# GpSimd's products two slots earlier in a pipelined block of attention, feed-forward and a selective scan, with a new table of places for the side work

## The chip, the cores and the metric

The kernel runs on one core of a Trainium2 chip. The metric is the device time of one launch in microseconds. Engines are named as in the profile: PE (TensorE), DVE (VectorE), ACT (ScalarE), POOL (GpSimd), SP (SyncE, which here only issues DMAs).

## What is computed

The input is 16 sequences of 512 tokens with 256 features. Each goes through four stages, each with a layer norm ahead and a residual behind. All but the scan can be cut to a few words; the scan sets the frame:

```python
x = x + attention(layernorm(x))      # 16 heads, squared scores, causal
x = x + int8_ffn(layernorm(x))
x = x + mamba_f(norm(x)) + mamba_b(norm(x) reversed)    # two directions
x = x + fp4_ffn(layernorm(x))        # blockwise quantised activations
...
def step(h, ins):                    # 512 inner features, 16 states, 512 tokens
    dt_t, u_t, B_t, C_t = ins
    h = jnp.exp(dt_t[..., None] * A) * h + (dt_t * u_t)[..., None] * B_t[:, None, :]
    y_t = jnp.einsum('bdn,bn->bd', h, C_t)
    return (h, y_t)
```

## The kernel before

One sequence at a time goes through the scan; its work is cut into 128 **slots**, one for each scan instruction of DVE (L1296, 128 features by 512 tokens). A slot belongs to direction r (0 forward, slots 0 to 63; 1 backward, 64 to 127), state s (four slots each, 32 states in all) and feature group m. Every engine runs its own program, slot by slot (`one(b)` on each engine); they meet at semaphores only. In each slot an engine does first its part of the scan and then its **side work**. The part of the scan, in slot j:

- SP issues the spread of row B of a state over all partitions (L688, `spread_b`), for the state of slot j + 7, into a ring of two buffers `bS`.
- POOL makes the products B * dt * u (L786, `inflow`), two slots' worth in one instruction, for slots j + 4 and j + 5. They go into a ring of four buffers `hb`, so the first one of state s waits until PE has transposed all of state s - 4 (`m_hT`).
- ACT makes the decay (L1017) of slot j + 2.
- DVE scans slot j.
- PE transposes the scanned state to token order (L1598, `turn_state`), one quarter per slot, 6 slots behind (slot j - 6), into two PSUM banks.
- DVE adds the first two quarters of each state into y (L1307) 7 slots behind; ACT multiplies the other two by C (L1025) 8 slots behind, and POOL adds them (L797, `add_last`) 9 slots behind.

Side work is everything else: attention and int8 feed-forward of the next sequence, fp4 feed-forward of the one before, the projections ahead of the scan and behind it. The table `PLAN`, filled by `row(piece, r, ahead, PE=[...], ACT=[...], ...)`, gives the slot of every part of a piece on each engine; the whole part of a number is the slot, and within a slot parts go by the number and then by the order of the rows. An engine takes its side work strictly in that order, and so a part that waits holds up all behind it, the next slot's part of the scan too.

Pieces that matter here: `p_in`, `p_conv` (projection and convolution, DVE L1250), `p_silu` (ACT L953 with a table load before and the load L837 behind), `p_x` (PE L1541, then the copy `xd`, ACT L962), `p_c`, `p_rows` (SP L677 writes `xd` out for the spreads) and `p_dt`: the step sizes, for each of four groups a product on PE (L1554), five instructions on ACT (L968 to L977), one on DVE (L1261) and three on POOL (L767, L770, L772). `p_du` is ACT L982. `q_gate`, `q_up`, `q_silu`, `q_hquant`, `q_htail`, `q_hturn`, `q_down` are the fp4 feed-forward (PE L1487, L1506, L1515; ACT L924, L928; DVE L1227, L1073 to L1084; POOL L741 to L747). The norms are `a_stat`/`a_norm` for attention, `f_` for int8, `m_` for the scan, `q_` for fp4: a statistic on DVE (L1124 to L1131), a root on ACT (L843, L845), four tiny instructions on DVE (L1137 to L1143, 128x4 elements) and four scalings on ACT (L851). `a_turn`, `a_k`, `a_v`, `a_q` (PE L1357, L1378, L1365, L1391) make the inputs of attention. `a_score` is PE L1411 and ACT L886, `a_mask` POOL L732. `i_turn`, `d_turn`, `d_gate`, `d_out` (PE L1560, L1570, L1579) close a direction.

## Time and profile before

| | us |
|---|---|
| median of 3 runs | 6269.05 (6259.05 to 6270.88) |
| profiled execution, its own time | 6267.12 |
| its span, first to last instruction | 6265.4 |
| busy: DVE, POOL, PE, ACT | 4807.9, 4688.4, 4489.1, 4183.9 |
| share of the span | 77%, 75%, 72%, 67% |
| mean granted clock of PE, full speed 1 | 0.864 |

A group row of the profile names the line, the engine, the operation and its tiles, then the count, the busy time and the mean duration in ns of one, and last the idle time of the engine before these instructions with what ended it. Nearly all buffers of the scan lie in `arena_m`, and those of the side work in `arena_a`, so lines tell more than tiles. Times in a timeline are from the span's start. The sequence used below begins its slot 0 at 2462.8 us and ends at 2838.4.

### The profile page before, as it was taken

How to read it: one execution, taken by the hardware profiler on the slowest of the kernel's cores; microseconds unless marked ns; L12 is line 12 of the kernel's file. 1: busy time of each engine (PE TensorE's matmuls, PEld its weight loads, DVE VectorE, ACT ScalarE, POOL GpSimd, SP SyncE). 2: the span in 40 equal slices, each digit the busy share in tenths (PEclk: the TensorE clock that was granted, in tenths of full speed). 3: DMA queues.
4: the chain of work that ended last, by engine and by line, in shares of the span. 5: the costliest groups of instructions: out<-in, count | busy, mean ns of one | idle time of the engine just before them, and what ended most of it. 6: DMA issues, size and time to landing. Idle time of an engine off the chain costs nothing. (4 is left out here: it accounts for less than half of the span.)

```text
span 6265.4 us, 79937 instructions
## 1 busy us (share of the span) xinstructions
PE 4489.1 (72%) x21853; PEld 2872.4 (46%) x21900; DVE 4807.9 (77%) x6052; ACT 4183.9 (67%) x7079; POOL 4688.4 (75%) x2442
## 2 busy tenths in 40 slices
...
GB/s 121 36 46 44 46 53 46 53 42 43 62 47 44 46 64 42 45 52 47 55 42 51 55 47 42 57 55 42 43 54 44 55 42 58 50 45 45 39 45 28
DMA packets 152786, 308.71 MB, mean 49 GB/s; under 512 B 20870, under 2 KB 58310, under 8 KB 149926
## 3 DMA queue, kind: packets, MB, share of 16 engines
...
q14 instruction: 294, 2.41, 0.1%
...
## 5 line engine op out<-in xcount | busy, mean ns | idle before, releaser
L786 POOL TENSOR_TENSOR arena_m<-bS,arena_m 128x1024 f32<-128x1024 f32 x1024 | 2429.0, 2383 | 400.6 <-PE psum L1598 349.2
L1296 DVE TENSOR_TENSOR_SCAN arena_m<-psum,arena_m 128x512 f32<-128x512 f32 x2048 | 2441.3, 1208 | 85.2 <-POOL arena_m L786 33.6
L1598 PE MATMUL psum<-ident,arena_m 128*128 128x128 f32 x8192 | 1426.2, 309 | 1020.4 <-ACT hc L1025 762.6
L1598 PEld LDWEIGHTS psum<-ident,arena_m 128*128 128x128 f32 x8192 | 1066.9, 158 | 1662.2 <-issue 889.8
L1017 ACT ACTIVATE psum<-arena_m,Aneg 128x512 f32<-128x512 f32 x2048 | 1400.2, 693 | 520.9 <-DVE arena_m L1296 508.2
L797 POOL TENSOR_TENSOR arena_m<-arena_m,hc 128x1024 f32<-128x1024 f32 x512 | 1213.6, 2370 | 307.3 <-ACT hc L1025 306.5
L1307 DVE SCALAR_TENSOR_TENSOR arena_m<-psum,Ct,arena_m 128x512 f32<-128x512 f32 x1024 | 751.8, 734 | 395.8 <-PE psum L1598 392.2
L1025 ACT ACTIVATE hc<-psum,Ct 128x512 f32<-128x512 f32 x1024 | 697.0, 681 | 62.3 <-PE psum L1598 61.5
L886 ACT ACTIVATE arena_a<-psum 128x512 f32<-128x512 f32 (+3 forms) x1024 | 386.4, 441 | 412.5 <-PE psum L1411 368.7
L1411 PE MATMUL psum<-arena_a 64*128 64x512 f32 (+3 forms) x2048 | 464.4, 559 | 190.9 <-ACT arena_a L886 78.2
L1487 PE MATMUL psum<-wB,arena_a 128*128 128x352 f32 x1024 | 396.4, 519 | 26.4 <-ACT arena_m L992 24.4
L732 POOL TENSOR_SCALAR_AFFINE_SELECT arena_a<-arena_a 128x512 f32<-128x512 f32 x256 | 161.3, 645 | 328.4 <-ACT arena_a L886 328.4
L1250 DVE SCALAR_TENSOR_TENSOR arena_m<-psum,convw,arena_m 128x509 f32<-128x509 f32 (+2 forms) x384 | 285.1, 742 | 130.6 <-ACT arena_m L948 122.6
L741 POOL TENSOR_TENSOR arena_a<-arena_a 128x704 f32<-128x704 f32 (+1 forms) x80 | 144.8, 1810 | 310.8 <-DVE arena_a L1084 310.8
L1411 PEld LDWEIGHTS psum<-arena_a 64*128 64x128 f32 x2048 | 204.2, 225 | 331.9 <-issue 133.3
L1261 DVE SCALAR_TENSOR_TENSOR arena_m<-psum,arena_m 128x512 f32<-128x512 f32 x128 | 88.0, 688 | 343.0 <-ACT arena_m L977 343.0
L1452 PE MATMUL psum<-arena_a,wA 128*128 128x512 bf16 x1105 | 285.4, 404 | 81.5 <-DVE arena_a L1189 74.8
L1524 PE MATMUL psum<-xnT,wU 128*128 128x512 f32 x512 | 265.6, 644 | 31.3 <-DVE arena_m L1250 28.4
L1579 PE MATMUL psum<-wO,arena_m 128*128 128x256 f32 x1024 | 249.8, 388 | 6.0 <-DVE xF L1279 1.7
L1487 PEld LDWEIGHTS psum<-wB,arena_a 128*128 128x128 f32 x1024 | 197.1, 212 | 115.6 <-issue 65.5
L1532 PE MATMUL psum<-xnT,wU 128*128 128x512 f32 x512 | 236.2, 594 | 0.3 <-ACT arena_m L992 0.3
L1515 PE MATMUL psum<-wA,arena_a 128*128 128x256 f32 (+1 forms) x768 | 219.5, 434 | 5.5 <-ACT arena_a L939 4.1
...
## 6 DMA issues: line engine op xcount, KB each, us to landing
bS<-brow SPq DMA_DIRECT2D x512, 256.0 KB, 3.3
...
```

The lines of the kernel that those rows point to most:

```text
L786: pool.tensor_tensor(hb[s % HBS][:, two, :], bS[:, s % 2, :].unsqueeze(1).to_broadcast([P, 2, T]), du[r][:, two, :], ALU.mult).then_inc(m_ ...
L797: pool.tensor_tensor(yT[:, 2:4, :], yT[:, 2:4, :], hc[:, s % 2, :, :], ALU.add).then_inc(m_yl.sem, 1)
L886: act.activation(asq[i][:, 2 * (j % 2) + j // 2, :], bank("a_score", None, w)[:, c:c + n], ACT.Square).then_inc(a_sq.sem, 1)
L1017: act.activation(EB[j % EBS], dt[r][:, m, :], ACT.Exp, scale=Aneg[:, r, m, n:n + 1]).then_inc(m_dA.sem, 1)
L1025: act.activation(hc[:, s % 2, i, :], HT[i], ACT.Copy, scale=Ct[:, r, 2 + i, n:n + 1]).then_inc(m_hc.sem, 1)
L1250: dve.scalar_tensor_tensor(u[:, m, late:T], src[:, 0:T - late], convw[:, r, m, tap:tap + 1], u[:, m, late:T], ALU.mult, ALU.add).then_inc( ...
L1296: dve.tensor_tensor_scan(v, EB[j % EBS], v, 0.0, ALU.mult, ALU.add).then_inc(m_scan.sem, 1)
L1307: dve.scalar_tensor_tensor(yT[:, i, :], HT[i], Ct[:, r, i, n:n + 1], yT[:, i, :], ALU.mult, ALU.add).then_inc(m_y.sem, 1)
L1411: ins = pe.matmul(bank("a_score", None, w - 1 + half)[:, c:c + n], kT[rows, ht, i * P:(i + 1) * P], qm[rows, j, i * P:T], start=True, stop ...
L1452: ins = pe.matmul(bank(piece, None, m), w[:, k, m * P:(m + 1) * P], xparts[:, c, k, :], start=(k == 0 and c == 0), stop=(k == KD - 1 and c ...
L1487: ins = pe.matmul(bank(piece, None, w)[:, 0:FIH], xTq[:, k, i * P:(i + 1) * P], w_[:, k, c * FIH:(c + 1) * FIH], start=(k == 0), stop=(k = ...
L1598: ins = pe.transpose(HT[i % 2][:, m * P:(m + 1) * P], hb[s % HBS][:, m, i * P:(i + 1) * P], ident[:, :])
```

## The change

Three things change in the frame: POOL's products are made for slots j + 6 and j + 7, the spread for the state of slot j + 9, and the table of the side work is new in nearly every row (the same pieces, the same counts, other slots). Two waits are added. Of the table these lines stand for the rest:

```diff
-        row("p_silu", 0, 1, ACT=[108])
+        row("p_silu", 0, 1, ACT=[105])
-        row("p_x", 0, 1, PE=[108, 108], ACT=[109])
+        row("p_x", 0, 1, PE=[105.4, 106], ACT=[107])
-        row("p_dt", 1, 0, PE=[35, 38, 41, 45], ACT=[37, 39, 43, 45], DVE=[37, 38, 44, 46], POOL=[40, 43, 47, 52])
+        row("p_dt", 1, 0, PE=[35, 36, 41, 44], ACT=[37, 39, 43, 45], DVE=[37, 39, 45, 45], POOL=[37, 40, 44, 49])
-        row("p_dt", 0, 1, PE=[111, 112, 113, 114], ACT=[112, 114, 114, 117.2], DVE=[113.1, 114.2, 116, 117], POOL=[114, 114.2, 117, 117])
+        row("p_dt", 0, 1, PE=[111, 113, 113.2, 114], ACT=[112, 112, 113, 118], DVE=[113, 113.2, 118, 119], POOL=[114, 115.1, 117, 122])
-        row("a_norm", None, 2, ACT=[118], DVE=[117])
+        row("a_norm", None, 2, ACT=[123], DVE=[119])
-        row("a_turn", None, 2, PE=[119, 120], ACT=[120, 121])
+        row("a_turn", None, 2, PE=[122, 123], ACT=[123, 124])
...
-                    sb_, jb = spot(b, j + 7)
+                    sb_, jb = spot(b, j + 9)
...
-                    ab, ja = spot(b, j + 4)
+                    ab, ja = spot(b, j + 6)
...
                 act.wait_ge(*m_dt_ps.by(moved(b, r - 1), NM * (2 - r)))
+                act.wait_ge(*m_ct_ps.by(moved(b, r - 1), 2 - r))
...
             def step_sizes(b, r, m):
+                pe.wait_ge(*m_xd.by(b, r + 1))
                 take_bank(pe, b, "p_dt", r, m)
```

Of the other pieces that are named below: `p_c` of direction 0 moves on PE from 111 to 108.1 and `p_rows` on SP from 121 to 107; `q_gate` on PE from 106, 107.1 (its last two) to 107, 107, `q_silu`'s last on ACT from 110 to 109, `q_up`'s last two on DVE from 109, 111 to 110, 111; `m_stat2` on DVE from 83, 85, 85 to 86, 87, 87; `q_norm` on DVE from 29 to 38; `l_x` on SP from 89 to 91; `a_mask` on POOL from 10, 17, 17, 19, 19 to 15, 16, 16, 17, 25 (its first five).

In the program after the change, lines from 961 on stand one lower than before, those from 1554 on two lower (L1017 is L1018, L1598 is L1600).

ACT, from the scan part of slot 106 to that of slot 108 before. L1017 and L1025 are the frame, L953 is `p_silu`, L962 the copy to `xd`:

```order
L1017 ACTIVATE psum<-arena_m,Aneg 128x512 x2
L1025 ACTIVATE hc<-psum,Ct 128x512
L1017 ACTIVATE psum<-arena_m,Aneg 128x512
L1025 ACTIVATE hc<-psum,Ct 128x512
L1017 ACTIVATE psum<-arena_m,Aneg 128x512
L924 COPY arena_a<-psum 128x352
L953 ACT_TABLE_LOAD
L953 ACTIVATE arena_m<-arena_m 128x2048
L837 ACT_TABLE_LOAD
L1017 ACTIVATE psum<-arena_m,Aneg 128x512
L962 COPY xd<-psum 128x512
```

ACT, slots 105 to 107 after:

```order
L939 COPY arena_a<-psum 64x128
L953 ACT_TABLE_LOAD
L953 ACTIVATE arena_m<-arena_m 128x2048
L837 ACT_TABLE_LOAD
L1018 ACTIVATE psum<-arena_m,Aneg 128x512
L1026 ACTIVATE hc<-psum,Ct 128x512
L1018 ACTIVATE psum<-arena_m,Aneg 128x512
L1026 ACTIVATE hc<-psum,Ct 128x512
L924 COPY arena_a<-psum 128x352
L963 COPY xd<-psum 128x512
```

The SiLU now stands ahead of the scan parts of slots 106 to 108 and of a copy of the fp4 gate (L924).

PE, the end of a sequence (slots 119 to 127) before. L1598 is the frame, four to a slot; L1357 is `a_turn`, L1378 `a_k`, L1365 `a_v`, L1391 `a_q`:

```order
L1357 MATMUL psum<-ident,arena_a 128x128 x4
L1598 MATMUL psum<-ident,arena_m 128x128 x4
L1357 MATMUL psum<-ident,arena_a 128x128 x4
L1378 MATMUL psum<-arena_a,wB 128x512 x2
L1598 MATMUL psum<-ident,arena_m 128x128 x8
L1378 MATMUL psum<-arena_a,wB 128x512 x2
L1598 MATMUL psum<-ident,arena_m 128x128 x4
L1365 MATMUL psum<-wB,arena_a 128x256 x8
L1598 MATMUL psum<-ident,arena_m 128x128 x4
L1391 MATMUL psum<-arena_a,wB 128x512 x2
L1598 MATMUL psum<-ident,arena_m 128x128 x12
L1391 MATMUL psum<-arena_a,wB 128x512 x2
```

PE, the end of a sequence (slots 122 to 126) after:

```order
L1358 MATMUL psum<-ident,arena_a 128x128 x4
L1600 MATMUL psum<-ident,arena_m 128x128 x4
L1358 MATMUL psum<-ident,arena_a 128x128 x4
L1379 MATMUL psum<-arena_a,wB 128x512 x2
L1600 MATMUL psum<-ident,arena_m 128x128 x4
L1366 MATMUL psum<-wB,arena_a 128x256 x4
L1379 MATMUL psum<-arena_a,wB 128x512 x2
L1600 MATMUL psum<-ident,arena_m 128x128 x4
L1392 MATMUL psum<-arena_a,wB 128x512 x2
L1600 MATMUL psum<-ident,arena_m 128x128 x4
L1366 MATMUL psum<-wB,arena_a 128x256 x4
L1392 MATMUL psum<-arena_a,wB 128x512 x2
```

The same products stood over nine slots, with eight groups of the frame between them, and now stand over five, with four.

POOL, the end of a sequence (slots 116 to 127) before; L786 is a product for two slots, L797 `add_last`, L767, L770 and L772 one group of `p_dt`:

```order
L797 TENSOR_TENSOR arena_m<-arena_m,hc 128x1024
L767 TENSOR_TENSOR arena_m<-arena_m 128x512
L770 TENSOR_TENSOR arena_m<-arena_m 128x512
L772 TENSOR_TENSOR arena_m<-arena_m 128x512
L767 TENSOR_TENSOR arena_m<-arena_m 128x512
L770 TENSOR_TENSOR arena_m<-arena_m 128x512
L772 TENSOR_TENSOR arena_m<-arena_m 128x512
L786 TENSOR_TENSOR arena_m<-bS,arena_m 128x1024 x2
L797 TENSOR_TENSOR arena_m<-arena_m,hc 128x1024
L786 TENSOR_TENSOR arena_m<-bS,arena_m 128x1024 x2
```

POOL, the same place after:

```order
L797 TENSOR_TENSOR arena_m<-arena_m,hc 128x1024
L767 TENSOR_TENSOR arena_m<-arena_m 128x512
L770 TENSOR_TENSOR arena_m<-arena_m 128x512
L772 TENSOR_TENSOR arena_m<-arena_m 128x512
L786 TENSOR_TENSOR arena_m<-bS,arena_m 128x1024 x2
L797 TENSOR_TENSOR arena_m<-arena_m,hc 128x1024
L786 TENSOR_TENSOR arena_m<-bS,arena_m 128x1024
L767 TENSOR_TENSOR arena_m<-arena_m 128x512
L770 TENSOR_TENSOR arena_m<-arena_m 128x512
L772 TENSOR_TENSOR arena_m<-arena_m 128x512
```

The last group of step sizes stands behind three products and one add that stood behind it, and each product in the row is one for slots two later than before.

## Rows read from the trace of the kernel before

**Rows 1.** Busy time of each engine over the sequence from 2463 to 2838 us

```profile
2463.00:2838.00 375.00, 273.51 (x1357) 175.33 (x1360) 298.70 (x373) 259.85 (x442) 293.92 (x153) 0.88 0.15 49
```

**Rows 2.** Groups of the whole span: busy us, mean ns, idle before

```profile
L1296 DVE TENSOR_TENSOR_SCAN arena_m<-psum,arena_m 128x512 f32<-128x512 f32 x2048 | 2441.3, 1208 | 85.2 <-POOL arena_m L786 33.6
...
L1137 DVE SCALAR_TENSOR_TENSOR lnv<-mv 128x4 f32<-128x4 f32 x80 | 88.5, 1106 | 6.4 <-ACT mv L845 6.4
```

**Rows 3.** POOL's waits in that sequence: us in total, times, longest

```profile
POOL arena_m L786 <- PE psum L1598: 21.2, 5, 6.6
POOL arena_m L797 <- ACT hc L1025: 19.1, 8, 5.2
...
POOL arena_m L786 <- DMA bS<-brow: 3.5, 1, 3.5
```

**Rows 4.** Timeline of ACT, slots 107 to 110: start, us, what, [idle before]

```profile
2770.36 0.69 ACT L1017 ACTIVATE psum<-arena_m,Aneg 128x512 f32<-128x512 f32 x1 [3.24 <-DVE arena_m L1296]
...
2773.94 1.91 ACT L953 ACTIVATE arena_m<-arena_m 128x2048 f32<-128x2048 f32 x1
2775.86 1.28 ACT L837 ACT_TABLE_LOAD   x1
...
2779.71 0.58 ACT L962 COPY xd<-psum 128x512 f32<-128x512 f32 x1 [1.86 <-PE psum L1541]
```

**Rows 5.** Timeline of DVE, slots 104 and 109

```profile
2762.05 2.31 DVE L1250 SCALAR_TENSOR_TENSOR arena_m<-psum,convw,arena_m 128x509 f32<-128x509 f32 x3 [0.69 <-ACT arena_m L948]
...
2783.97 0.53 DVE L1227 TENSOR_TENSOR arena_a<-psum,arena_a 128x352 f32<-128x352 f32 x1 [4.50 <-ACT arena_a L928]
```

**Rows 6.** Timeline of DVE, slots 38 and 46, the step sizes of direction 1

```profile
2571.12 0.69 DVE L1261 SCALAR_TENSOR_TENSOR arena_m<-psum,arena_m 128x512 f32<-128x512 f32 x1 [6.35 <-ACT arena_m L977]
...
2595.50 0.69 DVE L1261 SCALAR_TENSOR_TENSOR arena_m<-psum,arena_m 128x512 f32<-128x512 f32 x1 [7.66 <-ACT arena_m L977]
```

**Rows 7.** ACT's waits for PE in that sequence, and the one of slot 45

```profile
ACT arena_m L968 <- PE psum L1554: 4.4, 3, 1.8
...
2592.26 0.69 ACT L968 ACTIVATE arena_m<-psum,bdt 128x512 f32<-128x512 f32 x1 [1.30 <-PE psum L1554]
```

**Rows 8.** Timeline of POOL and DVE around slot 58, the norm `f_norm`

```profile
2598.97 2.37 POOL L797 TENSOR_TENSOR arena_m<-arena_m,hc 128x1024 f32<-128x1024 f32 x1 [5.19 <-ACT hc L1025]
...
2627.80 2.34 POOL L786 TENSOR_TENSOR arena_m<-bS,arena_m 128x1024 f32<-128x1024 f32 x1
2627.89 2.26 DVE L1143 SCALAR_TENSOR_TENSOR shift<-mv,ve 128x4 f32<-128x4 f32 x1
...
2635.74 2.36 POOL L786 TENSOR_TENSOR arena_m<-bS,arena_m 128x1024 f32<-128x1024 f32 x1 [5.61 <-PE psum L1598]
```

**Rows 9.** Timeline of DVE, slot 117, the norm `a_norm`

```profile
2813.48 1.13 DVE L1137 SCALAR_TENSOR_TENSOR lnv<-mv 128x4 f32<-128x4 f32 x1
2814.64 0.16 DVE L1139 TENSOR_TENSOR lnv<-lnv,ve 128x4 f32<-128x4 f32 x1
2814.84 1.12 DVE L1141 SCALAR_TENSOR_TENSOR ve<-lnv,mv 128x4 f32<-128x4 f32 x1
2815.99 1.19 DVE L1143 SCALAR_TENSOR_TENSOR shift<-mv,ve 128x4 f32<-128x4 f32 x1
```

**Rows 10.** Timeline of ACT and DVE: `a_norm`, slots 122 and 123, slot 0

```profile
2817.21 2.07 ACT L851 ACTIVATE arena_a<-xA,shift,ve 128x256 f32<-128x256 f32 x4 [2.41 <-DVE shift L1143]
...
2823.40 2.33 DVE L1296 TENSOR_TENSOR_SCAN arena_m<-psum,arena_m 128x512 f32<-128x512 f32 x2
...
2838.38 1.22 DVE L1296 TENSOR_TENSOR_SCAN arena_m<-psum,arena_m 128x512 f32<-128x512 f32 x1 [1.90 <-POOL arena_m L786]
```

**Rows 11.** Timeline of PE, slots 122 to 126

```profile
2826.30 1.88 PE L1378 MATMUL psum<-arena_a,wB 128*128 128x512 f32 x4
2828.01 0.60 PE L1598 MATMUL psum<-ident,arena_m 128*128 128x128 f32 x4
2828.45 3.62 PE L1365 MATMUL psum<-wB,arena_a 128*128 128x256 f32 x16
```

More of the change, by code:

```diff
@@ new lines, in block_kernel @@
+        row("a_qmask", None, 1, ACT=[24, 24.1, 26, 36])
+        row("q_stat", None, -1, ACT=[30.1], DVE=[26, 30, 30])
+        row("p_x", 1, 0, PE=[30, 30], ACT=[31])
+        row("p_c", 1, 0, PE=[34], DVE=[35])
+        row("p_dt", 1, 0, PE=[35, 36, 41, 44], ACT=[37, 39, 43, 45], DVE=[37, 39, 45, 45], POOL=[37, 40, 44, 49])
+        row("q_norm", None, -1, ACT=[65.1], DVE=[38])
+        row("p_du", 1, 0, ACT=[40, 51, 60, 61])
+        row("z_in", 0, 0, PE=[44, 45, 48, 50], ACT=[45, 46, 51.2, 52])
```

140 lines of the change are left out of this document (67 added, 73 removed).

## Prediction

> **What bounds the kernel now.** I read the busy time of a sequence first [rows 1]: in 375.0 us DVE is busy 298.7, POOL 293.9, PE 273.5 and ACT 259.9. None is above 80%, so no engine sets the pace alone. Then I read who waits for whom. Scans wait little: of 85.2 us of idle before 2048 scans, 33.6 are for the products that the change makes earlier [rows 2], or 2.1 us of the 374 or so that a sequence takes. POOL is mostly the one that waits: 21.2 us per sequence at a product for PE's transposes, 19.1 at an add for ACT [rows 3]. So an earlier product does not pay by itself. What is long is side work that stands in the way of its own consumer: DVE stands 4.50 us in slot 109 for a SiLU of the fp4 feed-forward [rows 5], 6.35 and 7.66 us in slots 38 and 46 for ACT's five instructions of a step size [rows 6]. The path goes back and forth between ACT, PE and DVE, and touches POOL only at the end of a sequence and where DVE's tiny norm instructions stretch: L1139 takes 0.16 us in slot 117 [rows 9], but L1137 has a mean of 1106 ns [rows 2], and in slot 58 L1143 starts 0.09 us after a POOL product and ends with it, 2.26 us [rows 8].
>
> The profiled execution took 6267.1 us, 2.0 under the median of 6269.05; I sum against 6267.1. The work is that of 16 sequences, one after the other, so a term per sequence counts 16 times.
>
> **The change, part by part.**
>
> *Direction 0's SiLU and step sizes, slots 104 to 112.* Before, the convolution ends on DVE at 2764.4 [rows 5], and the SiLU of its result runs only at 2773.9, behind ACT's slot 107. It and the two table loads take 1.91 + 2 x 1.28 = 4.5 us, then ACT waits 1.86 for PE's product of it [rows 4]. The fp4 SiLU for which DVE waits 4.50 us stands behind all this. After, the SiLU follows the convolution at once, where ACT idled 3.24 us for a scan [rows 4]. So 4.5 us of it lie over 3.24 of idle, 1.2 stick out, and the wait of 4.50 goes: -3.3. Bounds: 0, if PE, which now has the eight products of `p_x` ahead of four of the fp4 gate and up products, is late in its place, and -6.3 (4.5 + 1.86), if the whole block leaves the path. I take -3.3, which is nearest to the wait that a row shows.
>
> *Direction 1's step sizes.* PE's product for group 1 moves from slot 38 to 36, for group 3 from 45 to 44; ACT waited 1.8 and 1.30 us for these [rows 7], and DVE waited behind ACT. -3.1 at best, 0 if the scores which they pass now come late instead. I take the middle, -1.5. DVE's own part of group 1 moves from 38 to 39, which puts one scan ahead of the wait and saves nothing; `q_norm` moves into slot 38, that is, into the wait.
>
> *Products two slots earlier, spread nine ahead.* In POOL's idle of 5.19 us for an add [rows 8] one more product (2.34 us) fits. From there POOL worked without a pause until 2630.1, through all four norm instructions of slot 58, and then waited 5.61 us for PE, which had to wait for DVE. With one product less in that backlog POOL comes to its wait one product earlier, while DVE is in L1143, which then needs 0.16 us [rows 9] and not 2.26 [rows 8]. -2.1; bounds 0 (the backlog is still there: the last group of step sizes moved from 52 to 49 and the masks too, which changes no work but its order) and -4.2 (two instructions). I take -2.1. Scans' waits for products, up to -2.1, are left at 0, since they lie in the stretch of the next term. The spread keeps its distance to the product (three slots), so it costs nothing; behind `l_x`, which waits for POOL's `m_x`, now stands the spread of state 25 and not 24, and POOL's wait of 3.5 us for it [rows 3] goes. DVE did not wait there: 0.
>
> *The end of a sequence, slots 117 to 0.* `a_norm` moves from 118 to 123 on ACT, and everything behind it. Before, it began at 2817.2 and the next sequence's scan came 21.2 us later [rows 10]; the products in between could stretch over nine slots. After, it cannot begin before scan 122 is done (2824.5 in the time of before, with 13.9 us to go). Then come a decay and a scaling for the scan (1.3, two of L1017's size [rows 4]), `a_norm` 2.07 [rows 10], `a_turn` (1.8: four transposes like a group of the frame, 0.60, and two copies like L962's 0.58), both products of `a_k` at 1.88, `a_v` 3.62, one of `a_q` at `a_k`'s 1.88, three groups of the frame at 0.60 [rows 11], and DVE's copy of `a_v`, 0.7 like L1261 [rows 6]: 16.9 us. +3.0. Below it is bounded by -1.9, the scan's wait for POOL in slot 0 [rows 10], if DVE reaches slot 122 early, above by +3.0 and the stretch of the next term. POOL's last add of the direction, in slot 8, now has one more product ahead of it; it is covered by DVE's own lateness, and would cost 2.3 without that.
>
> *The four tiny instructions of `a_norm`*, on DVE from slot 117 to 119. They took 3.6 us beside POOL's short step-size instructions [rows 9]. Beside back-to-back products each takes up to 2.26 [rows 8], or 9.0. By the new order POOL is at its third group of step sizes about then, so I take no change; bounds -3.0 and +5.4.
>
> *Statistics.* `m_stat2` ends in slot 87, with its root and `m_norm2` in the same slot. 20 waits for a root cost 6.4 us [rows 2], 0.3 each; I take +0.5, between 0.3 and 1.0. The two added waits are for work that is long done or was waited for by `p_c` ahead of it: 0. All other places move by a slot or two both ways: 0, give or take 2.
>
> Sum per sequence: -3.3 - 1.5 - 2.1 + 3.0 + 0.5 = -3.4. Times 16: -54. 6267.1 - 54 = 6213.
>
> **The rivals.**
>
> *Slower: the end of a sequence.* PE's 11 us of attention inputs are pressed into five slots, and `a_norm` on DVE meets POOL's unbroken row of products: +3.0 + 5.4 + 0.5, against -3.3 and -2.1 elsewhere, and 0, its lower bound, for direction 1's step sizes: +3.5, or 6267 + 56 = 6323. It speaks for this that POOL has no pause there, and against it that POOL's place at that moment is its step sizes. It decides from the point where slots 117 to 0 lose more than the 6.4 us that the other terms gain.
> The Trainium skill has a rule that speaks for it ("SBUF — State Buffer", "Who interferes with whom"): a DVE instruction with two SBUF inputs and a GpSimd instruction that reads SBUF block each other for a whole instruction. All four instructions of a norm are of that kind, and the trace agrees (2.26 us beside a product, 0.16 without).
>
> *No change: given back.* The waits for ACT and PE go, and the next link is late by as much, since ACT, PE and DVE pass the work on in every slot; and a product cannot be earlier where it waits for PE's transposes in any case. 6267, within 12.
>
> *Much faster.* The SiLU's block leaves the path whole (-6.3), the step sizes give 3.1 and two norm instructions 4.2, and the end costs +3.0: -10.6, or 6267 - 170 = 6097.
>
> **How the numbers follow.** Forecast 0.44, much faster 0.12, no change 0.15, slower 0.29. A measurement of this kernel can tell 0.2%, 12.5 us, from no change. So faster 0.56, same 0.15, slower 0.29. The range goes from 6120, which leaves out most of the much faster case, to 6325, which takes the slower one in with its end.
>
> **What would show it.** The SiLU right behind the convolution and no wait of some 4 us in slot 109; ACT's L968 no longer waiting for PE in slots 39 and 45; L1143 in slot 58 at 0.2 us; PE without a pause from slot 122 to 127, and about 17 us from the end of scan 122 to the next sequence's first scan, where it was 13.9. I am wrong if `a_norm` on DVE takes 9 us, or if POOL's wait for transposes has grown at the places where its side work is waited for: with six slots ahead, a piece of side work in POOL's slot stands behind a product that may not start before PE's slot just ahead of it, and PE's weighing of values (slots 28 and 37) waits for masks that stand behind such a product.

## The result and the profile after

| | before | after |
|---|---|---|
| median, us (4 runs each) | 6264.05 (6256.76 to 6270.88) | 6185.4 (6177.17 to 6212.26) |
| ratio | 1 | 0.9882, 95% interval 0.9849 to 0.9915 |
| span of the profiled execution | 6265.4 | 6185.3 |
| busy: DVE, POOL, PE, ACT | 4807.9, 4688.4, 4489.1, 4183.9 | 4710.6, 4700.2, 4498.9, 4198.9 |
| granted clock of PE | 0.864 | 0.866 |

The change makes the kernel 1.2% faster, where 0.86% were forecast. The sign and the size were near. The experiments show that most of the reasons were not.

The sequence of after that answers to the one read before runs from 2444.7 to 2810.1 us, 365.4 us in place of 375.6. Its windows row (columns as in [rows 1]):

```profile
2444.70:2810.10 365.40, 271.88 (x1356) 175.43 (x1360) 292.36 (x374) 261.04 (x441) 293.81 (x154) 0.89 0.16 50
```

DVE is busy 6.3 us less [rows 1]. About half of it (52.7 us in the whole run, 3.3 per sequence) is the norms' four tiny instructions, the third most of all, which had a mean of 749 ns before (a group of the whole run, columns as in [rows 2]):

```profile
L1142 DVE SCALAR_TENSOR_TENSOR ve<-lnv,mv 128x4 f32<-128x4 f32 x80 | 16.1, 201 | 2.8
```

POOL's waits in that sequence, against [rows 3]:

```profile
POOL arena_m L786 <- PE psum L1600: 38.1, 12, 6.7
...
POOL arena_m L797 <- ACT hc L1026: 6.6, 3, 3.1
```

POOL waits 6.6 us for ACT at the add where it was 19.1, but 38.1 us for PE's transposes where it was 21.2. That is nearly the same idleness, moved to the product. The wait for the spread is gone.

The places that the prediction named. ACT around slots 105 to 109: the SiLU (L953) now stands earlier, and DVE in slot 110 takes the fp4 SiLU's result with no wait (before: 4.50 us [rows 5]).

```profile
2738.29 1.91 ACT L953 ACTIVATE arena_m<-arena_m 128x2048 f32<-128x2048 f32 x1
...
2747.93 0.45 ACT L924 COPY arena_a<-psum 128x352 f32<-128x352 f32 x1 [2.81 <-PE psum L1488]
...
2754.80 0.49 DVE L1228 TENSOR_TENSOR arena_a<-psum,arena_a 128x352 f32<-128x352 f32 x1
```

ACT's step sizes, L968 before [rows 7]: no wait at 2545 (slot 39), 0.77 where it was 1.30 in slot 45; in the sequence 1.4 us where it was 4.4.

```profile
2545.17 0.68 ACT L969 ACTIVATE arena_m<-psum,bdt 128x512 f32<-128x512 f32 x1
...
2568.23 0.69 ACT L969 ACTIVATE arena_m<-psum,bdt 128x512 f32<-128x512 f32 x1 [0.77 <-PE psum L1556]
```

DVE's norm `f_norm` in slot 58: 1.8 us for four instructions, and L1144 as short as forecast (2.26 before [rows 8]).

```profile
2599.85 1.25 DVE L1138 SCALAR_TENSOR_TENSOR lnv<-mv 128x4 f32<-128x4 f32 x1
2601.13 0.16 DVE L1140 TENSOR_TENSOR lnv<-lnv,ve 128x4 f32<-128x4 f32 x1
2601.33 0.16 DVE L1142 SCALAR_TENSOR_TENSOR ve<-lnv,mv 128x4 f32<-128x4 f32 x1
2601.53 0.16 DVE L1144 SCALAR_TENSOR_TENSOR shift<-mv,ve 128x4 f32<-128x4 f32 x1
```

DVE's norm `a_norm`, now in slot 119: 1.17 + 1.19 + 0.16 + 1.11 = 3.6 us, as in slot 117 before [rows 9].

```profile
2782.20 1.17 DVE L1138 SCALAR_TENSOR_TENSOR lnv<-mv 128x4 f32<-128x4 f32 x1
2783.40 1.19 DVE L1140 TENSOR_TENSOR lnv<-lnv,ve 128x4 f32<-128x4 f32 x1
2784.62 0.16 DVE L1142 SCALAR_TENSOR_TENSOR ve<-lnv,mv 128x4 f32<-128x4 f32 x1
2784.82 1.11 DVE L1144 SCALAR_TENSOR_TENSOR shift<-mv,ve 128x4 f32<-128x4 f32 x1
```

The end of the sequence, DVE and PE. From the end of scan 122 (2789.95) to the next first scan (2810.07) it is 20.1 us, where 17 were forecast; before, it was 13.8 (the prediction has 13.9) [rows 10]. The last down product of the fp4 feed-forward (L1516) now stands at its start, and DVE waits for PE:

```profile
2788.67 4.32 PE L1516 MATMUL psum<-wA,arena_a 128*128 128x256 f32 x12
...
2787.63 3.44 DVE L1297 TENSOR_TENSOR_SCAN arena_m<-psum,arena_m 128x512 f32<-128x512 f32 x3
2793.61 0.75 DVE L1308 SCALAR_TENSOR_TENSOR arena_m<-psum,Ct,arena_m 128x512 f32<-128x512 f32 x1 [2.55 <-PE psum L1600]
...
2810.07 1.22 DVE L1297 TENSOR_TENSOR_SCAN arena_m<-psum,arena_m 128x512 f32<-128x512 f32 x1 [2.57 <-POOL arena_m L786]
```

One place the prediction had priced at nothing. In slot 91 the scan's norm (`m_norm3`) takes 4.1 us, where it was 0.7. It falls beside the second of two POOL products and the add behind it, which now follow each other without a pause:

```profile
2684.95 4.67 POOL L786 TENSOR_TENSOR arena_m<-bS,arena_m 128x1024 f32<-128x1024 f32 x2 [0.75 <-PE psum L1600]
...
2688.21 1.43 DVE L1138 SCALAR_TENSOR_TENSOR lnv<-mv 128x4 f32<-128x4 f32 x1
2689.68 2.28 DVE L1140 TENSOR_TENSOR lnv<-lnv,ve 128x4 f32<-128x4 f32 x1
```

**Where a sequence's time went.** This table is worked out from the traces: the time from scan to scan, summed over stretches of slots, mean of 11 sequences (the fourth to the fourteenth). The first row is before, the others are differences to it, in us per sequence. The runs are those of the next section; e3 and e6, left out, differ from before by less than 1 us in every stretch. They do so by up to 0.9 us in slots 0 to 27 and 104 to 119, where they have no edit or gain nothing by it, so differences of that size in those stretches say nothing.

| slots | 0–27 | 28–31 | 32–39 | 40–55 | 56–63 | 64–75 | 76–87 | 88–91 | 92–103 | 104–111 | 112–119 | 120–127 | all |
|---|---|---|---|---|---|---|---|---|---|---|---|---|---|
| before | 73.8 | 11.3 | 26.0 | 41.1 | 23.3 | 37.2 | 35.2 | 9.0 | 39.5 | 28.9 | 30.6 | 18.3 | 374.2 |
| after | -3.0 | -3.2 | +0.3 | +3.6 | -6.6 | -0.4 | -1.4 | +4.3 | +0.7 | -2.8 | -2.2 | +5.8 | -4.9 |
| e1 | +0.3 | -2.5 | +2.6 | 0.0 | -0.9 | -0.1 | +2.1 | +3.5 | -0.8 | -0.3 | +2.7 | +0.4 | +6.9 |
| e2 | -3.0 | -3.1 | +0.5 | +2.9 | -6.5 | -1.0 | -3.0 | +4.7 | +3.1 | -3.8 | -2.4 | +6.1 | -5.5 |
| e4 | +0.8 | 0.0 | -1.3 | +5.1 | 0.0 | +2.8 | 0.0 | 0.0 | +0.1 | -0.1 | +0.1 | -0.2 | +7.2 |
| e5 | -1.9 | -3.4 | +0.2 | +4.6 | -6.6 | -0.4 | -1.4 | +4.3 | +0.7 | -2.8 | -3.0 | +6.7 | -3.0 |
| e7 | -1.4 | -3.0 | +0.1 | +2.6 | -6.6 | -0.9 | 0.0 | +3.0 | -0.2 | +0.2 | -0.4 | +0.2 | -6.4 |
| e8 | -0.8 | 0.0 | +0.2 | 0.0 | 0.0 | 0.0 | -3.0 | +4.7 | +4.1 | -4.1 | -2.6 | +6.0 | +4.4 |
| e9 | +0.3 | -2.5 | +2.6 | 0.0 | 0.0 | 0.0 | 0.0 | 0.0 | +0.1 | +0.4 | -0.4 | -0.1 | +0.4 |
| e10 | -0.3 | 0.0 | +0.1 | 0.0 | 0.0 | 0.0 | 0.0 | +4.7 | -1.2 | 0.0 | +1.1 | -0.2 | +4.3 |
| e11 | -2.8 | -2.9 | +0.1 | +2.1 | -6.7 | -0.5 | -2.0 | +6.1 | -0.5 | 0.0 | +0.5 | -0.1 | -6.6 |
| e12 | -2.5 | -3.3 | +0.1 | +3.5 | -6.4 | -2.4 | -3.0 | 0.0 | +4.1 | -2.5 | -1.6 | +6.6 | -7.1 |

### The profile page after: what moved, and what is told of

Its sections match the earlier page's. It is cut to its first block, busy times and chain, and to the rows that moved or that the text cites. A ratio compares the mean times of both kernels' runs of the same rounds, so it can differ in the third digit from the quotient of the medians.

```text
span 6185.3 us, 80047 instructions
## 1 busy us (share of the span) xinstructions
PE 4498.9 (73%) x21838; PEld 2895.5 (47%) x21900; DVE 4710.6 (76%) x6052; ACT 4198.9 (68%) x7079; POOL 4700.2 (76%) x2442
## 4 chain that ended last, share of the span: by engine, by line
PE 40%; DVE 22%; issue 15%; ACT 13%; POOL 8%; DVEq 1%; DMA 1%; ACTq 0%; POOLq 0%; SPq 0%
PE psum L1600 7%; DVE arena_m L1297 7%; PE psum L1412 5%; PE psum L1453 4%; PE psum L1581 4%; DVE arena_m L1251 3%; POOL arena_m L786 3%; PE psum L1470 3%; DVE arena_m L1308 3%; PE psum L1488 2%; PE psum L1525 2%; ACT psum L1018 2%; PE psum L1516 2%; ACT arena_a L886 2%; PE psum L1424 2%
## 5 line engine op out<-in xcount | busy, mean ns | idle before, releaser
L786 POOL TENSOR_TENSOR arena_m<-bS,arena_m 128x1024 f32<-128x1024 f32 x1024 | 2405.5, 2367 | 686.6 <-PE psum L1600 680.0
L1600 PE MATMUL psum<-ident,arena_m 128*128 128x128 f32 x8192 | 1428.0, 309 | 853.1 <-ACT hc L1026 647.6
L1600 PEld LDWEIGHTS psum<-ident,arena_m 128*128 128x128 f32 x8192 | 1089.2, 159 | 1504.5 <-issue 724.5
L1018 ACT ACTIVATE psum<-arena_m,Aneg 128x512 f32<-128x512 f32 x2048 | 1411.1, 693 | 449.1 <-DVE arena_m L1297 447.6
L797 POOL TENSOR_TENSOR arena_m<-arena_m,hc 128x1024 f32<-128x1024 f32 x512 | 1231.8, 2406 | 159.6 <-ACT hc L1026 117.6
L1412 PE MATMUL psum<-arena_a 64*128 64x512 f32 (+3 forms) x2048 | 433.4, 526 | 212.9 <-DVE arena_m L1262 84.5
L732 POOL TENSOR_SCALAR_AFFINE_SELECT arena_a<-arena_a 128x512 f32<-128x512 f32 x256 | 162.3, 646 | 200.1 <-ACT arena_a L886 198.3
L1525 PE MATMUL psum<-xnT,wU 128*128 128x512 f32 x512 | 266.3, 645 | 34.6 <-DVE arena_m L1251 33.8
L1533 PE MATMUL psum<-xnT,wU 128*128 128x512 f32 x512 | 252.9, 623 | 20.4 <-ACT arena_m L993 17.9
L1556 PE MATMUL psum<-xd,wdtT 128*128 128x512 f32 x256 | 185.4, 816 | 78.4 <-DVE arena_m L1262 58.8
```

The source lines that it names most:

```text
L786: pool.tensor_tensor(hb[s % HBS][:, two, :], bS[:, s % 2, :].unsqueeze(1).to_broadcast([P, 2, T]), du[r][:, two, :], ALU.mult).then_inc(m_ ...
L797: pool.tensor_tensor(yT[:, 2:4, :], yT[:, 2:4, :], hc[:, s % 2, :, :], ALU.add).then_inc(m_yl.sem, 1)
L1018: act.activation(EB[j % EBS], dt[r][:, m, :], ACT.Exp, scale=Aneg[:, r, m, n:n + 1]).then_inc(m_dA.sem, 1)
L1412: ins = pe.matmul(bank("a_score", None, w - 1 + half)[:, c:c + n], kT[rows, ht, i * P:(i + 1) * P], qm[rows, j, i * P:T], start=True, stop ...
L1600: ins = pe.transpose(HT[i % 2][:, m * P:(m + 1) * P], hb[s % HBS][:, m, i * P:(i + 1) * P], ident[:, :])
```

## The experiments

| run | what | median, us | ratio to before, 95% interval |
|---|---|---|---|
| e1 | old table, six slots ahead | 6367.1 | 1.0168 (1.0147 to 1.0188) |
| e2 | new table, four slots ahead | 6167.0 | 0.9826 (0.9805 to 0.9846) |
| e3 | before, SiLU of direction 0 earlier | 6275.1 | 1.0012 (1.0003 to 1.0022) |
| e4 | before, products of step sizes earlier | 6370.4 | 1.0158 (1.0144 to 1.0172) |
| e5 | after, attention's inputs at old places | 6191.0 | 0.9879 (0.9862 to 0.9897) |
| e6 | before, POOL's last step sizes at 49 | 6264.5 | 1.0004 (0.9995 to 1.0013) |
| e7 | e2, new rows only to slot 66 | 6172.1 | 0.9854 (0.9840 to 0.9868) |
| e8 | e2, new rows only behind slot 66 | 6322.1 | 1.0093 (1.0078 to 1.0109) |
| e9 | before, `q_norm` at 38 | 6259.5 | 0.9998 (0.9989 to 1.0007) |
| e10 | before, `l_x` at 91 | 6329.7 | 1.0108 (1.0092 to 1.0123) |
| e11 | e2, new rows only to slot 84 | 6154.9 | 0.9824 (0.9807 to 0.9841) |
| e12 | e2, `l_x` at 89 | 6142.4 | 0.9803 (0.9785 to 0.9820) |

Each ratio is to runs of the kernel before on the same chip (medians of 6262 to 6268).

### e1 and e2: the lookahead and the table, each alone

```diff
-                    ab, ja = spot(b, j + 4)
+                    ab, ja = spot(b, j + 6)
...
```

(e1, against before. With it the spread goes from j + 7 to j + 9, and `p_rows` of direction 0 on SP from 121 to 112. e2, against after, takes the products and the spread back to j + 4 and j + 7.)

> The kernel before with its own table, but GpSimd's products for slots j + 6 and j + 7 and the spread for the state of slot j + 9; direction 0's row write p_rows moves on SP from 121 to 112, since the earlier spread needs it. Before is 6264 us. Theory one (the earlier products are worth 2.1 us per sequence, by the one norm instruction in slot 58 that no longer meets a product, and they need no new table): 6264 - 34 = 6230, and L1143 in slot 58 takes 0.2 us. Theory two (the two parts work together only: by itself the lookahead puts the side work of GpSimd, which kept its slots, behind products that wait for TensorE's transposes): 6264 or slower, up to 6320, and GpSimd's wait of L786 for L1598 grows from 349 us to over 600. Theory three (the table does it all): 6264 within 12.

> The changed kernel with its new table, but the products again for slots j + 4 and j + 5 and the spread for slot j + 7. Before is 6264 us, after 6185. Theory one (the two parts add, the table's places are worth 45 us and the lookahead 34): 6219, and the norm of slot 58 has one instruction of about 2 us again. Theory two (the new table was made for the earlier products; GpSimd's last step sizes of direction 0 in slot 122 and the norms' new places need them): 6264 or slower. Theory three (the table does it all): 6185 to 6195.

e1 is 1.7% slower (its theory two), e2 1.7% faster, and faster than after itself, whose interval (0.9849 to 0.9915) lies just above e2's. So the table alone makes the gain, and the earlier products take some of it back: 0.6% by the ratios, 18 us or 0.3% by the medians. None of the theories for e2 had it faster than after. By the table of stretches `f_norm` in slots 56 to 63 is as short in e2 (-6.5) as in after (-6.6), and hardly shorter in e1 (-0.9): the lookahead is not its cause.

What six slots cost: the waits of POOL over the whole run of e1 (before: 349.2 and 306.5 us).

```profile
POOL arena_m L786 <- PE psum L1598: 749.6, 278, 12.2
...
POOL arena_m L797 <- ACT hc L1025: 86.0, 103, 4.4
```

The ring of four buffers holds 16 slots. A product for slot j + 6 needs the transposes of slot j - 7, which PE makes in its slot j - 1, just ahead; for slot j + 4 they are those of j - 9, and three slots of slack are left. In slots 86 to 88 of e1, POOL waits 3.74 us (3.73 before), and then has two products and an add in a row, where before it had one product and the add. The norm in slot 87 falls beside them: its L1139 takes 2.26 us and not 0.16, 2.1 us, which is the +2.1 of slots 76 to 87.

```profile
2749.09 4.66 POOL L786 TENSOR_TENSOR arena_m<-bS,arena_m 128x1024 f32<-128x1024 f32 x2 [3.74 <-PE psum L1598]
...
2753.80 2.26 DVE L1139 TENSOR_TENSOR lnv<-lnv,ve 128x4 f32<-128x4 f32 x1
```

The other two large losses of e1 are not that norm. In slots 88 to 91 (+3.5) the mean granted clock of PE is 0.60, where before has 1.00, DVE waits 1.87 us for PE, and the norm takes 1.7 us where it was 0.7. In slots 112 to 119 (+2.7) POOL waits some 7 us for a spread, which stands on SP behind the loads of attention's weights; over the run its waits for spreads are 93.4 us, where before has 50.5. How much of each comes from the six slots, and how much from `p_rows` in its new place, was not tried.

### e3: direction 0's SiLU, the prediction's first term

```diff
-        row("p_x", 0, 1, PE=[108, 108], ACT=[109])
+        row("p_x", 0, 1, PE=[105.4, 106], ACT=[107])
-        row("p_silu", 0, 1, ACT=[108])
+        row("p_silu", 0, 1, ACT=[105])
```

> The kernel before with one block moved: direction 0's SiLU on ACT from 108 to 105, the eight products of p_x on TensorE from 108 to 105.4 and 106, the copy xd on ACT from 109 to 107. All else as before. Before is 6264 us. Theory one (the term of the prediction: 3.3 us per sequence, since the wait of 4.5 us of DVE in slot 109 goes): 6264 - 53 = 6211. Theory two (the block is shifted, not saved, because ACT's scan parts and the copy of the fp4 gate now stand behind 4.5 us of SiLU and table loads, and p_c and the step sizes keep their places): 6264 within 12, with the wait turning up in slots 105 to 108 for ACT L1017 or PE.

Theory two holds: nothing is gained (the interval even has it 0.03 to 0.22% slower). The SiLU ends early, and DVE in slot 109 still waits 3.81 us of the 4.50. On ACT the fp4 SiLU (L928) stands in slot 110, behind that slot's decay, and the decay waits for DVE's scan. First ACT, then DVE:

```profile
2791.60 0.69 ACT L1017 ACTIVATE psum<-arena_m,Aneg 128x512 f32<-128x512 f32 x1 [2.17 <-DVE arena_m L1296]
...
2794.55 0.79 ACT L928 ACTIVATE arena_a<-arena_a 128x704 f32<-128x704 f32 x1
...
2795.37 0.53 DVE L1227 TENSOR_TENSOR arena_a<-psum,arena_a 128x352 f32<-128x352 f32 x1 [3.81 <-ACT arena_a L928]
```

From the end of scan 109 (2791.56) to the end of the SiLU (2795.34) ACT works without a pause: the decay, the scaling by C, a copy of the gate, the table load and the SiLU. DVE waits in slot 109 for a thing that ACT does in slot 110, which itself waits for scan 109. In the new table `q_silu` is at 109 and `q_up` on DVE at 110, and the wait is gone. That this swap is the cause is argued from these rows; it was not tried alone.

### e4: direction 1's step sizes, the second term

```diff
-        row("p_dt", 1, 0, PE=[35, 38, 41, 45], ...
+        row("p_dt", 1, 0, PE=[35, 36, 41, 44], ...
```

> The kernel before with TensorE's products for direction 1's step sizes of groups 1 and 3 in slots 36 and 44 in place of 38 and 45. Before is 6264 us. Theory one (the term of the prediction, 1.5 us per sequence, at best 3.1): 6264 - 24 = 6240, down to 6214. Theory two (as with direction 0's SiLU, which alone gave nothing: a single wait taken away is given back by the next link in the round of ACT, TensorE and DVE): 6264 within 12; the waits of ACT's L968 for TensorE go all the same.

Neither theory: it is 1.6% slower. The rows show the chain behind most of it. The table also hands out three PSUM banks, and group 1's product has the bank of group 0. So in slot 36 it waits 2.46 us for DVE to read group 0 (PE, L1554). Everything on PE behind it is late, so POOL waits 3.30 for transposes, its masks (L732) come late, PE waits 3.14 for them at its weighing (L1423), which then takes 4.49 us, and DVE waits 5.41 us for the transposes behind that. Before, PE waited 0.89 us there and the same 32 products took 2.36 us. The difference of 2.1 us is the clock: the granted clock during them was 1.00 before and is 0.50 in e4.

```profile
2608.36 1.52 PE L1554 MATMUL psum<-xd,wdtT 128*128 128x512 f32 x2 [2.46 <-DVE arena_m L1261]
...
2610.82 2.35 POOL L786 TENSOR_TENSOR arena_m<-bS,arena_m 128x1024 f32<-128x1024 f32 x1 [3.30 <-PE psum L1598]
...
2615.42 1.22 POOL L732 TENSOR_SCALAR_AFFINE_SELECT arena_a<-arena_a 128x512 f32<-128x512 f32 x2
...
2616.77 4.49 PE L1423 MATMUL psum<-arena_a,vx 128*32 128x512 f32 x32 [3.14 <-POOL arena_a L732]
...
2629.74 0.75 DVE L1307 SCALAR_TENSOR_TENSOR arena_m<-psum,Ct,arena_m 128x512 f32<-128x512 f32 x1 [5.41 <-PE psum L1598]
```

In the new table the masks move too: the last two ahead of that weighing stand in POOL's slot 36 and not 40, with the weighing in 37 and not 39. Slots 36 to 47, 3.7 us longer in e4, are 1.3 shorter in after, with the same early products. That the masks are the reason was not tried alone, and the +2.8 of slots 64 to 75 in e4 stays unexplained.

### e5: attention's inputs back at their old places

```diff
-        row("a_norm", None, 2, ACT=[123], DVE=[119])
-        row("a_turn", None, 2, PE=[122, 123], ACT=[123, 124])
+        row("a_norm", None, 2, ACT=[118], DVE=[117])
+        row("a_turn", None, 2, PE=[119, 120], ACT=[120, 121])
...
```

(`a_k`, `a_v` and `a_q` likewise.)

> The changed kernel with the end of a sequence as before: a_norm, a_turn, a_k, a_v and a_q at their old slots (a_norm on ACT 118 and DVE 117, a_turn on TensorE 119 and 120, a_k 120 and 122, a_v 123, a_q 124 and 127). After is 6185 us. By the traces, slots 120 to 127 of after take 5.8 us per sequence more than before, and slot 119's norm on DVE 3.5 us where slot 117's was 3.6. Theory one (the pressed end costs the 3.0 us of the prediction, or the 5.8 that the traces differ by): 6185 - 48 = 6137, down to 6092. Theory two (what the end loses is what slots 116 to 119 gain, -5.0 us, so that the old places give it back there; the step sizes of direction 0 and the norm then stand in each other's way again): 6185 within 12, with slot 117 at 9 us.

The same as after, so theory two's time, though the norm in slot 117 takes 4.0 to 5.1 us and not 9. Slots 120 to 127 are still 6.7 us longer than before's. The fp4 feed-forward's last down product, in PE's slot 121 where it was 118, now falls between the two halves of `a_k`, and DVE waits 6.89 us in slot 123. The first half of `a_k` takes 3.17 us just ahead of it, at a granted clock of 0.61; the second, at full clock, 1.88. First PE, then DVE:

```profile
2794.73 3.07 PE L1516 MATMUL psum<-wA,arena_a 128*128 128x256 f32 x12
...
2798.43 0.75 DVE L1308 SCALAR_TENSOR_TENSOR arena_m<-psum,Ct,arena_m 128x512 f32<-128x512 f32 x1 [6.89 <-PE psum L1600]
```

So the new places of attention's inputs are not what makes the end long. What is left are the other rows of the table there: the later down product, which stands in the way by these rows, but also the last of `q_hturn` (120 where it was 115) and of the step sizes (POOL 122 where it was 117). None was tried alone. The clock has a part in it too: over slots 120 to 127 the mean granted clock is 0.99 before and 0.87 to 0.88 in every version with the new places there (after, e2, e5, e8, e12).

### e6: the place of POOL's last step sizes

```diff
-        row("p_dt", 1, 0, ..., POOL=[40, 43, 47, 52])
+        row("p_dt", 1, 0, ..., POOL=[40, 43, 47, 49])
```

> The kernel before with one number changed: GpSimd's three instructions for direction 1's last group of step sizes in slot 49 (so ahead of the product of slot 50, by GpSimd's steps of two) in place of 52. Theory one (what made slot 58 short in the changed kernel is not the products' lead but this place: GpSimd is through its backlog before the norm of the int8 feed-forward comes on DVE, which then takes 2 us and not 7.7): slots 56 to 63 take 4 to 7 us per sequence less, and the time is 6264 - 16 x 3 to 6 = 6168 to 6216, if nothing is given back. Theory two (the prediction's term, which put the gain to the lookahead and nothing to this place): 6264 within 12, and slot 58 as before. Theory three (it goes, and the next link takes it back by slot 70): slot 58 short and 6264 within 12.

Theory two's time and its unchanged slot 58: slots 56 to 63 did not change by a tenth of a microsecond. But the lookahead, to which theory two gives the gain, had been ruled out by e2. The move changes the order of POOL's work and not its sum, and so it left the backlog as it was. What e2's trace shows at slot 58 is a coincidence in time: POOL waits 0.73 us for ACT before its add of slot 60, and three of the norm's instructions fall into that pause.

```profile
2598.08 2.36 POOL L797 TENSOR_TENSOR arena_m<-arena_m,hc 128x1024 f32<-128x1024 f32 x1 [0.73 <-ACT hc L1026]
...
2597.40 0.16 DVE L1140 TENSOR_TENSOR lnv<-lnv,ve 128x4 f32<-128x4 f32 x1
```

In e2 the norm begins 1.2 us ahead of the end of POOL's product for slots 64 and 65, in before 3.2 us ahead of it, and there POOL's add follows with no pause; three of the four instructions then take 2.3 us each. Which of the first half's rows shifts it stays open.

### e7 and e8: halves of the table

```diff
-        row("f_gate", None, 1, PE=[66, 67, 68, 68, 70.1, 71.2], ...
+        row("f_gate", None, 1, PE=[66, 67, 68, 68, 70.2, 70.3], ...
...
```

(e7: every row from `f_gate` on as before. e8: every row ahead of it as before. The loads go with their half.)

> New places for the side work of slots 0 to about 66 alone (every row of the table up to f_rest, and the loads l_X 1, l_g0, l_Z 0, l_O 0), the old places behind, products four slots ahead as before. The whole new table with four slots ahead took 6167 us, and by its trace it is 9.2 us per sequence ahead of before when slot 64 begins, and 5.5 at the end. Theory one (the gain is made in the first half and part of it lost in the second): 6264 - 16 x 9.2 = 6117. Theory two (each stretch's time hangs on what the one before left behind, and the halves belong together): 6167 or more, with slots 64 to 80 longer than before's.

> The other half: the rows from f_gate on, and the loads of slots 55 to 126, at their new places, those of slots 0 to about 66 at the old ones, four slots ahead. By the trace of the whole new table with four ahead, slots 64 to 127 take 3.7 us per sequence more than before's. Theory one (halves add): 6264 + 59 = 6323. Theory two (the second half of the table has gains of its own, slots 72 to 79 and 104 to 119 for instance, and its losses in 88 to 103 and 120 to 127 come from arriving early): 6264 or less.

e8 came out at 6322, 1 us from its theory one. The stretches of e8 behind slot 76 repeat those of e2 to a few tenths (but for 1.0 in slots 92 to 103), although slots 0 to 63 are those of before. So most stretches do add here. The first half has the gain, the second half costs. But e7 is 6172 and not 6117: 3.0 us of the missing 3.4 per sequence went in slots 88 to 91, where its rows are those of before. Mostly for that reason the whole does not add: e7 and e8 together give -2.0 us per sequence, e2 has -5.5.

What happens in slots 88 to 91 can be read within e7 itself. In seven of the eleven sequences the norm of slot 91 takes 0.7 us, as before, and the granted clock is 1.00. In the other four it takes 6.3 to 6.6 us, and the clock is 0.50: PE is late, DVE waits 1.87 us for it, and the norm misses POOL's pause. These are two sequences of e7, one of each kind, each from some 1.5 us behind the start of scan 88 (columns as in [rows 1]; the column behind the busy times is the granted clock):

```profile
2299.30:2306.30 7.00, 5.50 (x12) 3.24 (x13) 6.21 (x13) 3.31 (x7) 4.65 (x2) 0.50 0.35 101
2675.00:2682.00 7.00, 4.52 (x20) 2.59 (x20) 6.93 (x16) 4.90 (x12) 4.66 (x2) 1.00 0.35 96
```

### e9: `q_norm` alone

```diff
-        row("q_norm", None, -1, ACT=[67], DVE=[29])
+        row("q_norm", None, -1, ACT=[67], DVE=[38])
```

> The kernel before with one number changed: the four tiny instructions of the fp4 feed-forward's norm (q_norm) on DVE in slot 38 in place of 29. In slot 29 they take 1.9, 2.3, 0.2 and 0.2 us beside GpSimd's products; in slot 38 DVE stands 6.35 us for the step sizes in any case, and the norm is put ahead of that wait. Theory one (the gain of the first half of the new table in slots 24 to 31, 3.0 us per sequence, is this move alone, and it is not given back): 6264 - 16 x 3.0 to 4.6 = 6190 to 6216. Theory two (like the other single moves, it is given back, here at once in slots 38 to 46): 6264 within 12.

Theory two, though the gift is given back sooner than it says: -2.5 us in slots 28 to 31, +2.6 in 32 to 39. DVE comes early and waits 1.35 and 2.46 us for PE, where before it had no wait over 0.5 in slots 30 to 32; PE has the eight products of `p_x` (L1541) there. First PE, then DVE:

```profile
2545.89 3.70 PE L1541 MATMUL psum<-arena_m,wO 128*128 128x512 f32 x8 [0.21 <-ACT arena_a L886]
...
2545.72 0.75 DVE L1307 SCALAR_TENSOR_TENSOR arena_m<-psum,Ct,arena_m 128x512 f32<-128x512 f32 x1 [1.35 <-PE psum L1598]
...
2550.06 0.75 DVE L1307 SCALAR_TENSOR_TENSOR arena_m<-psum,Ct,arena_m 128x512 f32<-128x512 f32 x1 [2.46 <-PE psum L1598]
```

Nothing is left at the end: the norm's time lay over a time in which DVE would have waited for PE in any case.

### e10: the load `l_x` alone

```diff
-        row("l_x", None, 2, SP=[89])
+        row("l_x", None, 2, SP=[91])
```

> The kernel before with one number changed: the load l_x on SP in slot 91 in place of 89, behind the spread of state 24 and not ahead of it. GpSimd then no longer waits 3.5 us for that spread in slot 92. Theory one (that pause of GpSimd is what lets the scan's norm in slot 91 through: in every kernel that has l_x at 91, slots 88 to 91 take 4.3 to 4.7 us per sequence more, since two tiny instructions take 2.3 us each beside products): 6264 + 16 x 4.4 = 6334, with the norm in slot 91 at over 4 us. Theory two (the prediction's 0 for this: DVE did not wait there): 6264 within 12. Theory three (a wait less is a gain): under 6252.

6330 where theory one said 6334. On SP the side work of a slot stands ahead of its spread, other than on the engines that compute. So before, POOL stands 3.49 us in slot 92 for the spread of state 24, which is queued behind `l_x`, and the four instructions of the norm take 0.16 us each in that pause (before, POOL and DVE):

```profile
2720.32 2.36 POOL L786 TENSOR_TENSOR arena_m<-bS,arena_m 128x1024 f32<-128x1024 f32 x1 [3.49 <-DMA bS<-brow]
...
2718.72 0.16 DVE L1139 TENSOR_TENSOR lnv<-lnv,ve 128x4 f32<-128x4 f32 x1
```

With `l_x` behind the spread the pause is gone, the products follow each other, and the same instructions last until a POOL instruction ends (e10):

```profile
2745.12 4.66 POOL L786 TENSOR_TENSOR arena_m<-bS,arena_m 128x1024 f32<-128x1024 f32 x2
2749.73 2.36 POOL L797 TENSOR_TENSOR arena_m<-arena_m,hc 128x1024 f32<-128x1024 f32 x1
...
2749.84 2.27 DVE L1139 TENSOR_TENSOR lnv<-lnv,ve 128x4 f32<-128x4 f32 x1
2752.14 2.26 DVE L1141 SCALAR_TENSOR_TENSOR ve<-lnv,mv 128x4 f32<-128x4 f32 x1
```

L1139 ends at 2752.11, and POOL's add at 2752.09. One number in a table, a wait removed on an engine that was not late: 1.1% slower. This bears out the rule of the Trainium skill that the prediction cites ("SBUF — State Buffer", "Who interferes with whom").

### e11 and e12: versions that could beat both

```diff
-        row("m_stat2", None, 1, ACT=[87], DVE=[86, 87, 87])
+        row("m_stat2", None, 1, ACT=[87], DVE=[83, 85, 85])
...
```

(e11, against e2: `m_stat2` and every row behind it, and the loads, as before; `f_gate` to `q_turn` stay new.)

```diff
-        row("l_x", None, 2, SP=[91])
+        row("l_x", None, 2, SP=[89])
```

(e12, against e2: this line alone.)

> New places from slot 0 to about 84 (all rows up to f_down and q_turn), the old ones behind, l_x at 89 among them, products four slots ahead. The version with the new places to slot 66 took 6172 us. Theory one (stretches add: slots 76 to 79 gain 2.8 us per sequence, and the losses of the new places in slots 96 and 120 to 127 are not there): 6172 - 45 = 6127. Theory two (the arrival at slot 84 is set by something else, or the pause of GpSimd that lets the norm of slot 91 through is lost, 4.4 us per sequence): 6172 to 6200.

> The whole new table with products four slots ahead (6167 us) and one number put back: the load l_x on SP in slot 89, where the kernel before has it, in place of 91. Theory one (what the kernel before lost by the opposite edit, 4.2 us per sequence, is won here: GpSimd then waits some 3.5 us for the spread of state 24, and by the trace of 6167 us the norm of slot 91 begins 1.7 us after the start of that wait and needs 0.7 us in it): 6167 - 67 = 6100, with the norm in slot 91 at under 1 us and slots 88 to 91 at 9 to 10 us in place of 13.7. Theory two (as with the version with new places to slot 84: the norm comes too late for the pause and meets the two GpSimd instructions behind it): 6167 to 6210, slots 88 to 91 at 14 us or more. Theory three (a wait put back is a loss): 6167 + 56.

e11 took 6155 us, 17 less than e7 where theory one gave 45. Slots 88 to 91 are 6.1 us longer than before's, although `l_x` is at 89 and POOL has its pause. The norm misses it. DVE's add ahead of it waits 1.59 us for PE, and the second tiny instruction runs into the product that ends the pause:

```profile
2667.75 0.75 DVE L1308 SCALAR_TENSOR_TENSOR arena_m<-psum,Ct,arena_m 128x512 f32<-128x512 f32 x1 [1.59 <-PE psum L1600]
...
2668.60 2.35 DVE L1140 TENSOR_TENSOR lnv<-lnv,ve 128x4 f32<-128x4 f32 x1
```

PE was late by its clock, as in four sequences of e7. These are the windows around it in e11, and below them those of before:

```profile
2656.00:2660.00 4.00, 1.48 (x10) 0.94 (x8) 3.52 (x6) 1.87 (x4) 1.48 (x1) 1.00 0.00 2
2660.00:2668.00 8.00, 6.49 (x19) 4.02 (x20) 6.38 (x14) 5.08 (x12) 4.66 (x2) 0.58 0.46 130
```

```profile
2708.00:2712.00 4.00, 1.29 (x9) 0.80 (x7) 3.52 (x6) 2.06 (x4) 1.29 (x1) 1.00 0.01 2
2712.00:2720.00 8.00, 5.21 (x23) 3.09 (x24) 7.84 (x19) 5.88 (x13) 4.66 (x2) 1.00 0.50 147
```

In before the granted clock of these 8 us was 1.00 (2.4 GHz), in e11 0.58, nearly half, with the same instructions in the same order. In the 4 us ahead PE was busy 1.48 us in e11 and 1.29 in before, at full clock in both. In all eleven sequences of e11 the clock there is 0.56 to 0.76 and the norm takes 2.9 to 7.1 us. Why the clock falls in one kernel and not in the other stays open.

e12 has the lowest median of the study, 6142 us, 2.0% faster than before; its lead over e2 is not clear of noise (0.9785 to 0.9820 against 0.9805 to 0.9846). Slots 88 to 91 are back at before's 9.0 us, as theory one has it, and the norm stands in the pause (POOL, then DVE):

```profile
2672.17 2.36 POOL L786 TENSOR_TENSOR arena_m<-bS,arena_m 128x1024 f32<-128x1024 f32 x1 [3.40 <-DMA bS<-brow]
...
2670.47 0.15 DVE L1138 SCALAR_TENSOR_TENSOR lnv<-mv 128x4 f32<-128x4 f32 x1
2670.66 0.16 DVE L1140 TENSOR_TENSOR lnv<-lnv,ve 128x4 f32<-128x4 f32 x1
```

But against e2 it gained 25 us by the medians and not 67. Of the 4.7 us per sequence, 1.0 went back in slots 92 to 103, 1.4 in 104 to 111, 0.8 in 112 to 119 and 0.5 in 120 to 127. Slots 0 to 87 are 0.6 us shorter in sum, slots 64 to 75 alone 1.4, for which this edit gives no reason.

## Why the prediction was right, and where it was not

The sum was -3.4 us per sequence, the traces give -4.9. That the two are near is luck, as the steps show one by one:

- **Direction 0's SiLU, -3.3.** Slots 104 to 111 gained 2.8 in after, and the wait in slot 109 went, as foretold. The reason was wrong: e3 moves just this block and gains nothing. The step that failed is "the fp4 SiLU for which DVE waits 4.50 us stands behind all this". It stood behind a decay that waited for the scan: of the 4.50 us the block made 0.7, and 3.81 are left without it. The release that ended last was not followed back to the queue it came from. What gave the 2.8 us, the swap of `q_silu` and `q_up` most likely, was not tried alone.
- **Direction 1's step sizes, -1.5, bounds -3.1 to 0.** Alone they cost 7.2 (e4). The waits of ACT in rows 7 did shrink, from 4.4 to 1.4 us per sequence, but "0 if the scores which they pass now come late" was not the lower bound. The bank, shared with the group before, was never looked at.
- **Products two slots earlier, -2.1 by `f_norm`.** Slots 56 to 63 gained 6.6 us, three times as much, L1144 at 0.16 us as foretold, and none of it by the lookahead (e2 has 6.5 without it). The mechanism, tiny instructions that meet or miss a POOL product, was right, its cause and its size were wrong. The lookahead itself costs: 1.7% with the old table (the move of `p_rows` that it needs included), 0.3 to 0.6% with the new one. The prediction's own sign of being wrong, a grown wait of POOL for transposes, came true: 680.0 us over the run in after, 349.2 before.
- **The spread, 0.** The prediction had POOL's wait of 3.5 us for it go, and priced that at 0, since "DVE did not wait there". This is the worst step, +4.3 us per sequence in slots 88 to 91 (e10: 67 us of the run by this one place). In six of the eleven sequences of after some 1.9 us of it are a wait for PE at a granted clock of 0.52; the norm itself takes 3.9 to 4.1 us in all. The wait of one engine was the cover under which another's norm ran. The prediction used that very mechanism for slot 58 and did not ask it of slot 91. By e10 and e12 the loss of the pause came from `l_x` on SP, which the prediction had named.
- **The end of a sequence, +3.0.** +5.8 in slots 120 to 127, right in sign, half the size. Of its parts, the pressing of attention's inputs was not the cause (e5). The down product that moved from 118 to 121, 4.32 us on PE, was missing in the sum, and so was the clock; how they share the rest was not tried. Slots 112 to 119, which it left, are 2.2 shorter.
- **`a_norm` on DVE, 0.** Right: 3.6 us in both.
- **Statistics, +0.5.** Slots 84 to 87 are 1.5 longer in after, but 0.1 shorter in e2 with the same table. So it is not the root, but the lookahead: the norm in slot 87 takes 2.4 us in after and 0.8 in e2.
- **All others, 0 within 2.** Slots 0 to 31 gained 6.1 us, 32 to 55 gave 3.9 back, 76 to 87 gained 3.0 in e2. None was in the sum, nor was `q_norm`, whose four instructions took 4.6 us in slot 29; by e9 its move is worth nothing alone.

The forecast was right in sign and near in size by luck: large terms that it lacked nearly cancel, the gain in slots 0 to 63 (8.9 us with `f_norm`'s), and the losses in slots 88 to 91 and 120 to 127. The rival "slower" had its price from the end and from GpSimd's instructions holding up a norm. Both came about, with +5.8 and +4.3, the second at another norm: `a_norm` took 3.6 us and not 9. What outweighed it was the first half of the table, as e7 and e8 show.
